# Layer 1's leaky relu as one ScalarE pass and a VectorE maximum, with four logit products a quad in place of eight

## The reference

```python
xl = (h @ lin_l_w.T + lin_l_b).reshape(n, h_heads, c)      # 8 heads of 16
xr = (h @ lin_r_w.T + lin_r_b).reshape(n, h_heads, c)
e = (edge_attr @ lin_edge_w.T).reshape(-1, h_heads, c)
z = jax.nn.leaky_relu(xl[src] + xr[dst] + e, NEG_SLOPE)    # NEG_SLOPE = 0.2
logits = jnp.einsum('ehc,hc->eh', z, att)
...
alpha = num / den[dst]                                     # softmax over the edges of a node
attn_out = jax.ops.segment_sum(xl[src] * alpha[..., None], dst, num_segments=n)
```

## Time and profile before

| what | value |
|---|---|
| median of 3 runs | 2989.43 us |
| lowest and highest | 2985.38, 2994.2 us |
| the profiled execution | 2994.84 us |
| its span, first to last instruction | 2993.0 us |
| TensorE clock granted, mean | 0.826 |
| layer 0 | 0 to about 1477 us |
| layer 1's edges, from the first to the last leaky relu | 1477 to about 2825 us |
| the last quads' sums | to about 2869 us |
| MLP and norms | to 2993 us |

### The profile page before, as it was taken

The page is one execution under the profiler, slowest core; times in us unless marked ns, Lnnn a source line. Parts: engine busy times, 40 slices in busy tenths (PEclk is TensorE's granted clock), DMA queues, the critical chain, the costliest instruction groups (busy, mean ns, idle before and its releaser), DMA issues. The chain is left out here.

```text
span 2993.0 us, 52671 instructions
## 1 busy us (share of the span) xinstructions
PE 2201.2 (74%) x14461; PEld 1756.5 (59%) x14461; DVE 1718.3 (57%) x7092; ACT 1126.6 (38%) x2973; POOL 1725.0 (58%) x1739
## 2 busy tenths in 40 slices
PE   7766665666666666667578888887888887888779
PEld 5665665665555666556355555555555665656556
DVE  2355555555555555557346656666666666666766
ACT  2355555555555555555333222222222222222123
POOL 3356666666666666655565656666666666666322
PEclk9687788788788877887788888987888888888879
DMA  5344444444444444432644444444444444444201
GB/s 136 97 117 111 109 112 105 113 113 109 109 111 114 106 112 112 123 88 59 171 148 141 147 142 126 144 143 140 144 146 147 144 131 139 146 146 147 62 20 36
DMA packets 378501, 356.41 MB, mean 119 GB/s; under 512 B 61695, under 2 KB 335743, under 8 KB 371424
## 3 DMA queue, kind: packets, MB, share of 16 engines
q1 hardware_dynamic: 314640, 236.51, 28.3%
q0 software_dynamic: 53248, 109.16, 14.2%
q10 hardware_dynamic: 10320, 7.37, 0.9%
HBM read 338.98 MB, written 13.82 MB: 118 GB/s over the span
## 5 line engine op out<-in xcount | busy, mean ns | idle before, releaser
L846 POOL DMA_INDIRECT rows<-xl_tab,src_cols x832 | 844.0, 1014 | 505.9 <-issue 228.1
L279 POOL DMA_INDIRECT rows<-in_x,src_cols x832 | 796.6, 957 | 537.0 <-issue 208.9
L330 PE MATMUL tile_sums<-gather,rows 128*128 128x128 f32 x1664 | 420.1, 342 | 254.4 <-DVE node_sums L560 172.4
L560 DVE TENSOR_TENSOR node_sums<-node_sums,tile_sums 128x256 f32 x832 | 350.0, 421 | 387.1 <-PE tile_sums L332 182.9
L330 PEld LDWEIGHTS tile_sums<-gather,rows 128*128 128x128 f32 x1664 | 322.9, 241 | 296.7 <-issue 190.1
L320 PE MATMUL p_dst<-window,spread 128*128 128x129 f32 x1664 | 331.1, 333 | 200.9 <-issue 154.1
L1022 DVE SCALAR_TENSOR_TENSOR node_sums<-node_sums,shrunk,tile_sums 128x128 f32 x832 | 280.7, 337 | 238.2 <-remote 175.6
L320 PEld LDWEIGHTS p_dst<-window,spread 128*128 128x128 f32 x1664 | 283.6, 241 | 219.8 <-issue 207.6
L332 PE MATMUL tile_sums<-gather,ones 128*128 128x128 f32 x1664 | 389.8, 323 | 0.0
L548 DVE CUSTOM_DVE_ANT_0 product<-rows,p_dst 128x128 f32<-128x128 f32 x832 | 258.2, 348 | 226.3 <-remote 147.7
L909 PEld LDWEIGHTS z_ps<-spread,window 128*128 128x128 f32 x1664 | 254.6, 221 | 155.2 <-issue 132.9
(11 more groups left out here) (187 smaller groups left out, 2525.7 us busy)
## 6 DMA issues: line engine op xcount, KB each, us to landing
window<-p_tab SPq DMA_DIRECT2D x832, 64.5 KB
attr<-in_attrT SPq DMA_DIRECT2D x52, 1024.0 KB
window<-xr_tab SPq DMA_DIRECT2D x832, 64.0 KB
rel_bc<-rel_rows SPq DMA_DIRECT2D x208, 128.0 KB
rel_bc<-rel_rows SPq DMA_DIRECT2D x52, 512.0 KB
rows<-in_x,src_cols POOLq DMA_INDIRECT x832
rows<-xl_tab,src_cols POOLq DMA_INDIRECT x832
p_tab<-p_rows ACTq DMA_DIRECT2D x13, 258.0 KB, 3.5
```

The costliest lines, as they stand in the source:

```text
L279: nc.gpsimd.indirect_dma_start(out=rows[:, r, i, :], out_offset=None, in_=t["x"], in_offset=bass.IndirectOffsetOnAxis(ap=src_cols[:, tile: ...
L330: nc.tensor.matmul(tile_sums[k][:, i, 0, :], rows[:, Q % AHEAD0, 2 * k + i, :], gather1[:, Q % 2, 2 * k + i, :], start=True, stop=True)
L560: nc.vector.tensor_tensor(span, span, tile_sums[i // 2][:, i % 2, :, :], ALU.add).then_inc(added, 1)
L846: nc.gpsimd.indirect_dma_start(out=rows[:, r, i, :], out_offset=None, in_=xl_tab, in_offset=bass.IndirectOffsetOnAxis(ap=src_cols[:, tile: ...
```

## The change

ACT makes 0.2 v alone, into half 0 of `z_act`. DVE then makes max(v, 0.2 v) into half 1, with v read from PSUM and its bias added in the same instruction; `z_bias`'s second column is therefore b in place of 0.8 b. PE multiplies half 1 alone: 4 products a quad. The semaphore `z_split` becomes `z_scaled` (ACT to DVE) and `z_maxed` (DVE to PE). The new `max_z(Q)` stands in DVE's step Q between `add_tile(A, 1)` and the group of operations that precede `add_tile(A, 2)`.

```diff
@@ scalar
-                def split_z(Q):
+                def scale_z(Q):
                     act.wait_ge(z_ready, Q + 1)
                     if Q >= 2:
                         act.wait_ge(lg_ready, Q - 1)
-                    nc.scalar.activation(z_act[:, Q % 2, 0, :], z_ps[Q % 2][:], ACT.Identity, bias=z_bias[:, 0:1], scale=0.2)
-                    nc.scalar.activation(z_act[:, Q % 2, 1, :], z_ps[Q % 2][:], ACT.Relu, bias=z_bias[:, 1:2],
-                                         scale=0.8).then_inc(z_split, 1)
+                    nc.scalar.activation(z_act[:, Q % 2, 0, :], z_ps[Q % 2][:], ACT.Identity, bias=z_bias[:, 0:1],
+                                         scale=0.2).then_inc(z_scaled, 1)
@@ tensor, make_z
                     if Q >= 2:
-                        pe.wait_ge(z_split, Q - 1)
+                        pe.wait_ge(z_maxed, Q - 1)
@@ tensor, make_logits
-                    pe.wait_ge(z_split, Q + 1)
+                    pe.wait_ge(z_maxed, Q + 1)
                     if q == 0 and s >= 2:
                         pe.wait_ge(lowered, s - 1)
-                    for part in range(2):
-                        for i in range(QT):
-                            lanes = slice(i * 32, i * 32 + 32)
-                            mm = nc.tensor.matmul(lg_ps[s % 2][lanes, 0, :], att_pad[:, q, :],
-                                                  z_act[:, Q % 2, part, i * P:(i + 1) * P],
-                                                  start=(q == 0 and part == 0), stop=(q == QUADS - 1 and part == 1),
-                                                  tile_position=(0, i * 32))
+                    for i in range(QT):
+                        lanes = slice(i * 32, i * 32 + 32)
+                        mm = nc.tensor.matmul(lg_ps[s % 2][lanes, 0, :], att_pad[:, q, :],
+                                              z_act[:, Q % 2, 1, i * P:(i + 1) * P], start=(q == 0),
+                                              stop=(q == QUADS - 1), tile_position=(0, i * 32))
                     mm.then_inc(lg_ready, 1)
@@ vector
+                def max_z(Q):
+                    dve.wait_ge(z_scaled, Q + 1)
+                    nc.vector.scalar_tensor_tensor(z_act[:, Q % 2, 1, :], z_ps[Q % 2][:], z_bias[:, 1:2],
+                                                   z_act[:, Q % 2, 0, :], ALU.add, ALU.max).then_inc(z_maxed, 1)
@@ vector, before the loop
-                nc.vector.tensor_scalar(z_bias[:, 1:2], b_cols[:, 0:1], b_cols[:, 1:2], 0.8, ALU.add, ALU.mult)
+                nc.vector.tensor_scalar(z_bias[:, 1:2], b_cols[:, 0:1], b_cols[:, 1:2], 1.0, ALU.add, ALU.mult)
@@ vector, in the loop
                     if adds:
                         add_tile(A, 1, bases[1])
+                    if Q < quads:
+                        max_z(Q)
                     if soft and q == 0:
                         find_seg_max(s)
```

More of the change, by code:

```diff
@@ L782, in build @@
         z_ready = sem("z_ready")
-        z_split = sem("z_split")
+        z_scaled = sem("z_scaled")
+        z_maxed = sem("z_maxed")
         lg_ready = sem("lg_ready")
@@ L886, in _ @@
                     if Q < quads:
-                        split_z(Q)
+                        scale_z(Q)
                     if Q % QUADS == 0 and 0 <= s - 1 < groups:
```

## The result

The changed kernel takes 3012.63 us (median of 5 runs, 3009.14 to 3018.35); the kernel before took 2994.17 us beside it (5 runs, 2985.38 to 2998.11). The ratio is 1.0076, 95% interval [1.0056, 1.0096]: slower by 0.76%, some 18 us. The prediction was 2922 us, faster. The direction was wrong. The time lies just inside the stated range of 2835 to 3015 us, in the part that was there for the slower case.

What follows compares the result with a forecast made beforehand. PE was taken to set layer 1's edge stage, by its own work and a starved stretch. Halved products -103 and -15 us, DVE's max_z +51: -67 us, giving 2922 us, with an 8-in-10 range of 2835 to 3015.

Steps and rivals of the forecast that it cites:

- What bounds the kernel: Layer 1's edge stage, 25.9 us a group of four quads, is set by PE: its own work and the starved stretch.
- starved stretch: One quad of four, where PE's logits come in bunches with 0.7 us "issue" gaps, taking 4.66 us instead of 0.58.
- (a) Halved products: Half the logits' products and loads go: -103 us in starved quads, -15 us in the quads behind them.
- low end: Starved-quad saving of 0: the stretch has its own length, and what follows the logits is starved instead.
- The sign named for it: If starved quads still take 9.8 us, the term that carries the gain is wrong.
- (b) ACT's second pass: Removing ACT's 0.678 us a quad is by itself worth nothing, since ACT is busy 23% of the stage.
- (c) `max_z`'s own time: The new DVE pass, 744 ns, holds DVE 0.66 us; two healthy quads a group rise 0.49 us each, +51 us.
- (d) Order and waits: DVE's 2.3 us from add_up's end through max_z, before the logits, is covered by PE's 2.38 us of make_z.
- each 0.1 us is 21 us: Cost over the stage of each 0.1 us of DVE's chain before the logits not covered by PE's make_z.
- Slower: Rival, chance 0.22: DVE's 19.95 us a group come on top of its 7.26 us of waiting; +68 us, 3057.
- The case of no gain: Rival, chance 0.10: PE's starved stretch is fixed in time and passes on to the tile sums; 0, 2990 us.
- The signs named beforehand: 1664 logit records, "issue" near 100 us, max_z 0.70-0.75 us, DVE busy +140, its waits some 280, healthy quads near 5.0 us.

Runs made afterwards that it cites:

- products_alone: Kernel before without ACT's second pass and the four products on it, nothing added on DVE; 2903.97 us, 0.9873 times before.
- pass_beside: Kernel before plus one 128x512 scalar_tensor_tensor on DVE at max_z's place, on a spare tile nobody reads; 2959.35 us, 1.0043 times before.
- early_both: Changed kernel with max_z ahead of DVE's wait for PE's sums and the spread made one quad earlier, three buffers; 2933.59 us, 0.9939 times before.
- early_max: Changed kernel with max_z moved from behind add_tile(A, 1) to right behind make_spread(Q + 1); 2938.84 us, 0.9972 times before.
- gathers_once_5: Kernel before with only the first 16 quads' gathers, reused: 2543.13 us beside 2939.01; as gathers_once 2346.16 us beside 2538.96.

## Why the prediction was wrong, step by step

**What bounds the kernel.** "So the stage is set by PE ... its own work, and the starved stretch" was wrong in its second half. A group's long quad is a standstill around late updates (`add_tile` waited "remote" 34 times in the stage, 5.2 us each, up to 9.0); PE's bunches fill it, they do not make it: in the changed kernel the update is as late while PE has nothing left to issue. The row was there: `add_tile`'s 7.26 us "remote" in the earlier trace rows, with 175.6 of 238.2 us "remote" in the earlier trace rows. I read it as DVE waiting for PE's slow instructions ("that wait is made of the very instructions that are halved"). It was not made of them: 239.7 us with half of them gone (products_alone).

**(a) Halved products, -103 and -15 us.** The sign was right and the size three times too large: 37 us measured, on chips where updates are late. That is nearer to what I had priced as the low end, a stretch with a length of its own. The sign named for it came in: counted from one quad's first product with w_e to the next, a tenth of the quads take 10.8 us or more in both kernels. Inside the changed kernel four more products cost 1.8% (the ratios 1.0271 and 1.0093, on two chips), some 50 us; PE, once held by `max_z`, has them on the path right behind the wait; that this is the reason is argued and not tried.

**(b) ACT's second pass, 0.** Not tried alone. products_alone holds it together with the products, so the 37 us are an upper bound for the products.

**(c) `max_z`'s own time, +51 us.** 738 ns a pass against 744 forecast. Its cost was put too high: 13 us in pass_beside (SBUF source, the same place). DVE absorbs most of it in idle time, and healthy quads did not go up by 0.49 us: counted as above, 145 quads before and 139 in the changed kernel take up to 7 us, 5.02 us on average in both. One pair of logits of the changed kernel shows how a quad without a late update goes, 5.31 us:

```profile
2178.06 0.43 PE L924 MATMUL lg_ps<-z_act,att_pad 128*32 128x128 f32 x8
...
2183.37 0.43 PE L924 MATMUL lg_ps<-z_act,att_pad 128*32 128x128 f32 x8
```

**(d) Order and waits, "covered with nothing to spare".** This is the step that turned the sign. I counted DVE's chain from the end of PE's record of `add_up`, 2.3 us, against PE's 2.38 us of `make_z`. The chain starts when DVE is told, and for that `add_tile` stood waiting up to 8.6 us. The sum of parts (-24 us) and the changed kernel (+0.93% of 2951, +27) leave about 51 us for it, over 52 groups one microsecond a group. This is an estimate across two chips, and the three intervals together allow some 17 us either way. Moving two lines took 1.2% back (again across two chips), and early_both 1.5% on one chip. PE's 267.8 us of waiting for `max_z`, where 14.9 are left in early_max, is the same step seen in the traces. The size fits what the record showed: my own "each 0.1 us is 21 us" was not the right unit, since only one quad of a group is late, by several microseconds, and a part of that would have been lost before as well, in bunches.

**The rivals.** "Slower" had the right place (DVE's step begins with a wait for PE's sums) and the right sign, but the price of 3057 us and its reason, DVE's time on top of its waiting, were wrong: DVE's time is the 13 us. What makes it slower is the queue position of a 0.74 us pass. I gave it 0.22. The case of no gain was nearest in time (2990).

**The signs named beforehand.** 1664 records, 0.738 us and 105.1 us of "issue" came in; DVE's waits on `add_tile` and `pick_grown` came to 364.8 us, not 280; DVE's busy time to +114 us up to 2826, where 11 us of the stage are still to come. Those that could have told right from wrong were the last two and PE's wait for z_act, forecast as small waits in healthy quads and found in few large ones.

**What stays open.** Why gathers make PE's updates late on the slow side and not on the quick one, whether it is the chip that makes the difference (two runs that name the same chip fell on different sides), and whether the recording of the trace has a part in it. The ends of PE's records are modelled, and the semaphore's own time (2170.24) says only when the news came, so how the 5.7 us split between a late end and a late update rests on the transposes that follow. What makes PE's bunches on the slow side is open too: instructions that arrive late are a rival that no run here excludes. A single ACT pass that makes the whole leaky relu, which would remove a pass and add none to DVE, was not tried.

## What to carry to other kernels

An operation placed behind a wait inherits that wait, and passes it on to whoever needs its result. Before a pass is moved to another in-order engine, look up the longest waits queued ahead of it, not the mean time between records, and put the pass ahead of them: here two lines moved were worth more than the change itself lost (1.0093 to 0.9972, and 0.9939 with the spread a quad earlier). Where an engine shows idle time marked "issue", ask what its neighbours wait for in the same microseconds before pricing its instructions: taking work out of a standstill that is set elsewhere gave a third of its price here. Measure both halves of an exchange separately, and on more than one chip: the same change was +0.9% on one side and nothing on the other. The version to keep is early_both, faster on both (0.9939 and 0.9968).

## What the runs showed of the hardware

- The same program takes about 2540 us in some places and 2939 to 2994 us in others. On the slow side `add_tile` on DVE stood up to 8.6 us at once for PE's update, as long as POOL gathered. Without gathers the two sides are alike: the stage takes 911.7 us (gathers_once_5), and on the quick side, by the row of gathers_once below, 895.8.

```profile
L857 ACT ACTIVATE z_act<-z_ps,z_bias x208: 662/687/690, 1279.8 to 2175.6; 128x512 f32<-128x512 f32 x104
```

- On the slow side the clock of the stage was 0.85 with gathers and 0.99 without (two chips), with the same work on PE and fewer standstills. Behind one standstill of 5.82 us the tile sums took 2.08 us, 1.16 ahead of it.
- In gathers_once_5 DVE's long waits, up to 10.3 us, end with the last gathers at 1529.5 us; behind them none is over 0.9 us.
- A scalar_tensor_tensor of 128x512 f32 with one source in PSUM takes 738 ns; 128x128 takes 334.
